# A transformer block on one core: in the middle stage, the weighted sums of one image are put ahead of the logits of the next

## The reference, cut to what matters

```python
    h = _L0_tok_ref(x, L0_tok_sqrt_eig, L0_tok_pct, 64)
    h = h + _L0_attn_ref(_layernorm(h, axis=-1), L0_attn_K, L0_attn_temperature, L0_attn_bias)
    h = h + _L0_ffn_ref(_layernorm(h, axis=-1), L0_ffn_W, L0_ffn_b)
...
        key = jnp.einsum('bsd,de->bse', x, K)
        logits = jnp.tanh(jnp.einsum('bsd,btd->bst', key, x) + bias[0])
...
        logits = logits - 10000.0 * (1.0 - band.astype(logits.dtype))
        logits = logits * temperature
        scores = jax.nn.softmax(logits, axis=-1)
        return jnp.einsum('bst,btd->bsd', scores, x)
```

## Time and profile before

| | before |
|---|---|
| median of 3 runs | 1486.73 us (1485.23 to 1488.94) |
| the profiled execution | 1486.39 us |
| its span, first to last instruction | 1484.3 us |
| TensorE busy | 1346.7 us (91%), mean granted clock 0.963 |
| VectorE busy | 930.7 us (63%) |
| ScalarE busy | 901.5 us (61%) |
| GpSimd busy | 550.5 us (37%) |
| keys of image 2 start, keys of image 63 start | 396.12 us, 1235.33 us |

### The profile page before, as it was taken

The page is one execution under the profiler, slowest core; times in us unless marked ns, Lnnn a source line. Parts: engine busy times, 40 slices in busy tenths (PEclk is TensorE's granted clock), DMA queues, the critical chain, the costliest instruction groups (busy, mean ns, idle before and its releaser), DMA issues. The chain is left out here.

```text
span 1484.3 us, 30741 instructions
## 1 busy us (share of the span) xinstructions
PE 1346.7 (91%) x8813; PEld 1166.9 (79%) x8813; DVE 930.7 (63%) x2025; ACT 901.5 (61%) x1956; POOL 550.5 (37%) x1390
## 2 busy tenths in 40 slices
PE   4999787776899999999999999999999997599993
PEld 3577665665899999999999999999999997355551
DVE  1132222222678878887887887888788786477771
ACT  1223222222577777777777777777777776467772
POOL 0000000000055555555555555555555555102222
PEclk8999999997999999999999999999999999699997
DMA  9979999997333333333333333233333322000000
GB/s 362 419 279 424 422 422 422 423 422 245 90 82 95 97 81 82 97 83 80 96 82 81 94 89 80 88 96 82 79 96 82 82 67 51 24 6 9 8 4 4
DMA packets 87990, 219.97 MB, mean 148 GB/s; under 512 B 20676, under 2 KB 33616, under 8 KB 75408
## 3 DMA queue, kind: packets, MB, share of 16 engines
q1 hardware_dynamic: 77456, 184.43, 38.3%
q10 hardware_dynamic: 5120, 33.56, 5.6%
q0 software_dynamic: 5376, 1.52, 0.6%
HBM read 148.16 MB, written 73.07 MB: 149 GB/s over the span
## 5 line engine op out<-in xcount | busy, mean ns | idle before, releaser
L192 PE MATMUL s1b<-pg,cg 128*128 128x256 f32 x1024 | 247.2, 401 | 65.6 <-DVE cg L156 64.9
L460 PE MATMUL ps_k<-sphi,Glo 128*128 128x256 f32 x1024 | 292.2, 285 | 0.0
L459 PE MATMUL ps_k<-splo,Ghi 128*128 128x256 f32 x1024 | 290.9, 284 | 0.0
L192 PEld LDWEIGHTS s1b<-pg,cg 128*128 128x128 f32 x1024 | 202.2, 201 | 112.3 <-issue 58.0
L458 PE MATMUL ps_k<-sphi,Ghi 128*128 128x256 f32 x1024 | 288.6, 282 | 0.0
L156 DVE TENSOR_TENSOR cg<-xg,se 128x1024 f32<-128x1024 f32 x64 | 78.1, 1225 | 219.9 <-DMA pg<-in_pct_dram 184.8
L243 ACT COPY stage<-s1b 128x512 f32<-128x512 f32 x128 | 74.4, 587 | 230.1 <-PE s1b L192 212.0
L779 POOL TENSOR_SCALAR ve<-var 128x2 f32<-128x2 f32 x64 | 14.0, 218 | 526.5 <-ACT squares L627 526.4
L458 PEld LDWEIGHTS ps_k<-sphi,Ghi 128*128 128x128 f32 x1024 | 194.6, 190 | 2.4
L459 PEld LDWEIGHTS ps_k<-splo,Ghi 128*128 128x128 f32 x1024 | 193.0, 189 | 2.7
L460 PEld LDWEIGHTS ps_k<-sphi,Glo 128*128 128x128 f32 x1024 | 193.7, 189 | 0.0
(11 more groups left out here) (141 smaller groups left out, 3089.0 us busy)
## 6 DMA issues: line engine op xcount, KB each, us to landing
pg<-in_pct_dram SPq DMA_DIRECT2D x64, 1024.0 KB, 26.2
xg<-in_xs_dram SPq DMA_DIRECT2D x64, 512.0 KB, 25.2
spec<-stage ACTq DMA_DIRECT2D x64, 512.0 KB, 8.1
xt<-spec SPq DMA_DIRECT2D x64, 512.0 KB, 5.4
out_dram<-o SPq DMA_DIRECT2D x64, 512.0 KB, 2.8
rrow<-rs SPq DMA_DIRECT2D x64, 128.0 KB, 4.7
recs<-rec SPq DMA_DIRECT2D x16, 160.0 KB, 5.4
recs<-rec,idx POOLq DMA_INDIRECT x128, 2.3
```

The lines of the kernel that those rows point to most:

```text
L192: last = nc.tensor.matmul(bank[(b % sets) * PARTS + part][:, m % 2, :], cg[:, b % SETS, m * 2 + h, :], pg[:, b, m * 2 + h, :], start=(h == ...
L459: nc.tensor.matmul(out_ap, whi, mlo, start=False, stop=False)
L460: last = nc.tensor.matmul(out_ap, wlo, mhi, start=False, stop=(j == n - 1))
```

## The change

Within a slot on TensorE, `attend(i-1)` is put ahead of `logits(i)`. Both keep their own waits, matmuls and semaphores; no other engine's list changes.

```diff
                 if has(i + 1):
                     inverse_dft(i + 1, (k + 1) % 4)
+                if has(i - 1):
+                    attend(i - 1, (k + 3) % 4)
                 if has(i):
                     logits(i, k)
-                if has(i - 1):
-                    attend(i - 1, (k + 3) % 4)
```

## The result

The changed kernel takes 1571.93 us (median of 4 runs, 1568.96 to 1575.81), against 1487.0 for the kernel before in the same comparison: a ratio of 1.0558, 95% interval 1.0534 to 1.0583. It is 85 us slower; forecast were 74 us, 1560. The profiled execution took 1573.16 us, its span is 1571.1.

The account below looks back on a forecast made before the run. TensorE was taken as the bound; a new loop of 0.20 + 8.98 + 0.10 + 2.75 + 2.88 = 14.91 us adds 70.3 us over 61 turns, the last logits 3.6: 1486.4 + 73.9, said as 1560 us, range 1548 to 1582.

Parts of the forecast that it names:

- What bounds the kernel: Middle stage: TensorE busy 150.00 of 150.00 us, turn 13.76 us; moving its work can't shorten it, only open gaps.
- the slack of lsc and of the sums: In each turn lsc had 1.73 us of slack against the logits, the sums 2.73 us against pTlo; the change spends both.
- The loop: Turns 2 to 63: end of logits, lsc, pTlo, waiting sums, logits again; 14.91 us a turn against 13.757, 70.3 us in all.
- release: On TensorE, from pTlo's end to the start of the sums that wait for it: 0.10 us a turn.
- The last logits: Turn 63, without inverse transform: lsc 14.21 us after the keys' start instead of 10.63, adding 3.58 us.
- the third rival: TensorE's clock drops because it now pauses in every turn: about 1875 us if every turn, 1591 if a tenth; chance 0.06.
- The sum: Whole kernel: 70.3 us for the loop plus 3.6 for turn 63 makes 73.9 us more, 1560 us.
- Only the direct wait: lsc and pTlo keep their place, sums wait 0.33 us a turn: 24 us more, 1510; chance 0.04.
- Not slower: lsc to pTlo shrinks by 1.23 us through h and its squares, turn stays 13.76, only turn 63 pays: 1490; chance 0.04.
- point of decision, 7.75 us: Time from lsc to pTlo at which sums find pTlo ready 8.05 us into the turn, which stays 13.76 us.
- The clock falls: Repeated TensorE pauses lower its clock to 0.62, 5.1 us a turn on top: about 1875 us, or 1591; chance 0.06.

Follow-up runs that it names:

- the kernel with both moves: Changed kernel with h and its squares moved ahead of lsc and tanh, and half of the logits ahead of the sums: 1484.69 us, 0.998 of the kernel before.
- the changed kernel once more: The changed kernel run again without further edits, as yardstick, compared with the kernel before: 1568.6 us, ratio 1.0537.
- h out of the chain: Changed kernel with the sums' scaling h moved ahead of lsc and its squares ahead of tanh, one turn earlier: 1513.58 us, 1.0171 of the kernel before.

## Why the prediction held, point by point

**What bounds the kernel.** Held: the slack of lsc and of the sums was both spent, and TensorE stopped being the bound. One premise was off: that moving the work about can't shorten it. The keys take 5.69 us where logits stand ahead of them and 5.77 where the sums do (last section); TensorE's own turn in the kernel with both moves is 13.66 us.

**The loop.** Held, step by step: lsc waits for the logits in every turn, pTlo follows a fixed time after lsc (but for every fourth turn), the sums wait for it, and ScalarE's idle time ahead of the second keyhi is gone. Its terms, forecast and measured in the turn above: keys' start to lsc 0.20 and 0.30; lsc to pTlo 8.98 and 8.83; release 0.10 and 0.19; sums 2.75 and 2.85 (the first matmul behind the pause takes 0.49 us instead of 0.40); logits 2.88 and 2.87. The sum was 14.91; over the 61 turns it was (1312.59 - 394.44) / 61 = 15.05, from the starts of the keys of images 2 and 63.

```profile
394.44 0.28 PE L458 MATMUL ps_k<-sphi,Ghi 128*128 128x256 f32 x1
...
1312.59 0.28 PE L458 MATMUL ps_k<-sphi,Ghi 128*128 128x256 f32 x1
```

That makes 8.6 us more than forecast, and it is a balance of errors that partly cancel. Mis-sized downward were the two hand-overs and the sums' first matmul. The release was read from a turn written out; the 0.20 was worked out from the last matmul's end and a hand-over between ScalarE and VectorE. Both hold in written-out turns to 0.01 us (0.20 and 0.11), but 52 turns run in the loop. Mis-sized upward was lsc to pTlo, by 0.15 us: in the earlier trace rows pTlo starts at 816.17, 0.11 behind the end of pThi (815.22 + 0.84 = 816.06), which the wait for the keys had made late. From splo's start to pTlo's end it is 2.75 us there and 2.61 in the changed kernel. So that wait did lengthen the chain that the prediction read, by way of pThi, though the prediction says that it doesn't; in the changed kernel it is gone. Every fourth turn's extra 0.21 us, some 2.7 us over the loop, was not in the 14.91 at all. That the forecast came within 1% is thus in part luck: the chain read too long paid for some of the hand-overs read too short.

**The last logits.** Forecast from the keys of image 63 to lsc were 14.21 us; it took 1328.37 - 1312.59 = 15.78. The sums started 8.30 us into that turn (8.38 forecast), but took 4.42 us instead of 2.75, for the clock fell. TensorE had paused for 1.98 us there, and in the window of these sums the granted clock is 0.62, so for part of it the lower level, 1.2 GHz (first TensorE, then VectorE's lsc, then the window, its columns as in the earlier trace rows):

```profile
1318.75 0.17 PE L502 MATMUL ps_l<-acc,ones 128*128 128x3 bf16 x1
1320.89 0.56 PE L458 MATMUL ps_av<-hhi,pThi 128*128 128x512 f32 x1 [1.98 <-issue]
...
1325.31 0.27 PE L458 MATMUL ps_l<-sphi,keyhi 128*128 128x256 f32 x1
```

```profile
1328.37 0.69 DVE L752 TENSOR_TENSOR lsc<-ps_l,rrow 128x512 f32<-128x512 f32 x1 [5.32 <-PE ps_l L460]
```

```profile
1320.80:1325.30 4.50, 4.41 (x12) 3.49 (x13) 2.18 (x6) 1.42 (x3) 3.27 (x8) 0.62 0.31 118
```

That is the third rival, in one turn of 64: 1.6 us. The pause alone doesn't decide it. The same 1.98 us stand ahead of the same sums in three more profiles: in two of them the sums are slow too (4.41 us with the changed kernel once more, 4.08 with h out of the chain), but with all turns written out the granted clock stays at 1.00, the sums take 2.84 us, and keys to lsc take 1310.50 - 1296.29 = 14.21 us, the forecast:

```profile
1296.29 0.28 PE L453 MATMUL ps_k<-sphi,Ghi 128*128 128x256 f32 x1
...
1304.59 0.47 PE L453 MATMUL ps_av<-hhi,pThi 128*128 128x512 f32 x1 [1.98 <-issue]
...
1307.43 0.28 PE L453 MATMUL ps_l<-sphi,keyhi 128*128 128x256 f32 x1
```

```profile
1310.50 0.69 DVE L747 TENSOR_TENSOR lsc<-ps_l,rrow 128x512 f32<-128x512 f32 x1 [3.75 <-PE ps_l L455]
```

```profile
1304.50:1307.50 3.00, 2.91 (x13) 2.43 (x14) 2.18 (x6) 1.42 (x3) 2.17 (x3) 1.00 0.23 86
```

What makes the difference was not tried.

**The sum.** From the first lsc to the last it is 863.7 us before (382.3 to 1246.0) and 947.5 after (380.9 to 1328.4): 83.8, of which 73.9 were forecast, 8.6 are the balance of the loop's terms and 1.6 the clock; 0.2 come off between the first lsc and the keys of image 2. The rest of the 86.8 us between the two profiles, 1.4 us less ahead of the first lsc and 4.4 more behind the last, is nothing that the forecast's steps contain.

**The rivals.** *Only the direct wait*: not what sets the turn here, as three logits ahead of the sums showed; but it is there beneath, at 14.10 us a turn. I had its price nearly right and treated it as a rival of the loop, where it is the next layer. *Not slower*: out, for lsc to pTlo stayed at 8.83 us. The edit that takes h out of the chain is this rival's own mechanism, made true by hand. Its point of decision, 7.75 us from lsc to pTlo, was wrong as a point at which the turn is 13.76 again, for pTlo also waits for this turn's keys. *The clock falls*: not in the steady turns. In 52 turns with a pause of some 1.1 us each (1.3 in every fourth) the granted clock stays 1.00. The Trainium skill's case of brief and frequent pauses that make the clock swing (TensorE: Matmul & The Clock Gate, "A second HAM failure mode: psum-queue depth-cycling") is not borne out by these 52 turns.

## What to carry to other kernels

Where the order on the busiest engine is changed, take every wait of the moved step and of the steps behind it back to what it hangs on, until the path comes round to the same engine: if a later input hangs on the output just delayed, the waits don't cost once but set a new period, the sum of the loop. Under the loop that you find stand others (here 15.04, 14.13, 14.10 and TensorE's own 13.66), so work out the next one before saying what a cure brings. And take the price of a hand-over from a turn that waits at the same step and is written in the same way, looped or unrolled: here the same two hand-overs cost 0.30 and 0.19 us in one, 0.20 and 0.11 in the other.

## What the runs showed of the hardware that was not expected

A wait on the path cost 0.19 us from pTlo's end to the sums' first matmul in the loop and 0.11 in turns written out, 0.30 and 0.20 from the keys' start to lsc; with the 52 turns of the loop written out the kernel is 12 to 15 us faster (1556.8 against 1568.6 and 1571.9). The profile shows no instruction for it, only idle time put down to "issue". The Trainium skill says why nothing is to be seen (Perfetto Trace Analysis, "Per-instruction lifecycle: what the profiler-reported window actually captures"): on every engine the wait for semaphores and the way of their signals lie outside the stretch that the profile shows of an instruction. The rows agree: the 0.19 us stand between two instructions, in neither. What costs the extra 0.09 us in the loop stays open. Counts from registers alone don't explain it: the hand-overs between VectorE and ScalarE have them too, and in three of four turns they cost the same in both kernels (lsc to the end of pTlo 8.83 us).

The 48 matmuls of the keys take 5.69 us where they follow logits (800.45 to 806.14, the same in all versions that were given a new order) and 5.77 where they follow the sums (808.77 to 814.54 before):

```profile
814.54 0.60 PE L482 MATMUL ps_pT<-ident,pr 128*128 128x128 f32 x4
```

That is 0.0017 us a matmul, spread over all of them, and most of what the best version gains in a turn (13.66 against 13.76). What it comes from was not tried.
